# Causal attention in one core: four narrow key tiles of the diagonal are packed in two pairs, and the probability ring grows from three buffers to five

## What is computed

```python
x = x + 0.5 * ffn(layernorm(x))      # 4096 tokens of 128 numbers; a router picks 1 of 8 experts for each
x = x + attn(layernorm(x))           # 4 sequences of 1024 tokens, 16 heads of width 8
x = x + 0.5 * ffn(layernorm(x))

q, k, v = heads(x @ Wq.T), heads(x @ Wk.T), heads(x @ Wv.T)
q, k = rope(q, pos), rope(k, pos)
score = einsum('bqd,bkd->bqk', q, k)
score = where(tril, score, -inf)
out = einsum('bqk,bkd->bqd', softmax(score / sqrt(8)), v) @ Wo.T
```

## Time and profile before

| | |
|---|---|
| median of 3 runs | 908.73 us (904.07 to 913.01) |
| the profiled execution, its own time | 911.38 us |
| its span from first to last instruction | 909.6 us |
| instructions | 17801 |
| mean granted TensorE clock | 0.926 |

### The profile page before, as it was taken

The page is one execution under the profiler, slowest core; times in us unless marked ns, Lnnn a source line. Parts: engine busy times, 40 slices in busy tenths (PEclk is TensorE's granted clock), DMA queues, the critical chain, the costliest instruction groups (busy, mean ns, idle before and its releaser), DMA issues. The chain is left out here.

```text
span 909.6 us, 17801 instructions
## 1 busy us (share of the span) xinstructions
PE 781.4 (86%) x5522; PEld 442.6 (49%) x5570; DVE 615.6 (68%) x1919; ACT 506.6 (56%) x1229; POOL 324.6 (36%) x606
## 2 busy tenths in 40 slices
PE   9757889988889999999999999999999876577795
PEld 8657778654323333333333333333333345476785
DVE  5625467569887788778877887788778419344463
ACT  2125456167337676767676767676767751154462
POOL 7253544546522233223322332233223310535543
PEclk8759899999779999999999999999999988689898
DMA  9511111206550332133213321332130010211100
GB/s 304 212 39 29 38 35 35 110 22 167 158 85 6 54 54 36 19 54 55 35 20 54 55 37 19 54 54 36 20 54 2 3 32 38 92 28 37 39 31 27
DMA packets 27990, 51.84 MB, mean 57 GB/s; under 512 B 7553, under 2 KB 19201, under 8 KB 26497
## 3 DMA queue, kind: packets, MB, share of 16 engines
q1 hardware_dynamic: 21296, 41.04, 19.6%
q0 software_dynamic: 4096, 8.69, 3.6%
q10 hardware_dynamic: 2512, 1.06, 0.5%
HBM read 35.40 MB, written 14.97 MB: 55 GB/s over the span
## 5 line engine op out<-in xcount | busy, mean ns | idle before, releaser
L1456 DVE CUSTOM_DVE_ANT_0 cst<-psS,mask_row 128x768 bf16<-128x768 f32 (+7 forms) x512 | 364.3, 756 | 93.1 <-PE psS L1316 90.6
L1420 ACT ACTIVATE prob<-psST 128x512 f32<-128x512 f32 (+3 forms) x750 | 316.8, 496 | 151.9 <-PE psST L1347 113.3
L1316 PE MATMUL psS<-ks,qs 125*128 125x512 bf16 (+3 forms) x768 | 190.6, 337 | 12.6 <-DVE a_rowmax L1456 12.0
L1347 PE MATMUL psST<-qs,ks 128*128 128x512 bf16 (+3 forms) x703 | 178.9, 324 | 5.3 <-issue 0.4
L1361 PE MATMUL a_psO<-prob,vs 128*32 128x512 f32 (+3 forms) x1536 | 164.1, 499 | 15.8 <-ACT prob L1420 14.6
L1540 POOL TENSOR_TENSOR a_gate<-a_zeros 1x1 f32<-1x1 f32 x128 | 23.4, 183 | 330.5 <-ACT prob L1420 330.5
L1316 PEld LDWEIGHTS psS<-ks,qs 125*128 125x128 bf16 x768 | 56.2, 98 | 162.2 <-DVE a_rowmax L1456 60.5
L1347 PEld LDWEIGHTS psST<-qs,ks 128*128 128x128 bf16 x750 | 68.5, 98 | 99.8 <-ACT prob L1420 49.0
L780 POOL DMA_INDIRECT tok<-rows,f_there_number x64 | 61.6, 963 | 102.0 <-DVE f_number L492 42.4
L729 ACT ACTIVATE f_xnT<-f_ps_half,gb 128x128 f32<-128x128 f32 x64 | 29.3, 457 | 114.2 <-PE f_ps_half L657 57.9
L666 PE MATMUL f_ps_wide<-f_xnT,f_w1s 128*128 x312 | 55.9, 307 | 41.4 <-issue 23.9
(11 more groups left out here) (181 smaller groups left out, 952.7 us busy)
## 6 DMA issues: line engine op xcount, KB each, us to landing
qs<-q_split SPq DMA_DIRECT2D x96, 96.0 KB
rows<-tok SPq DMA_DIRECT2D x8, 536.0 KB, 4.8
ks<-k_split SPq DMA_DIRECT2D x32, 128.0 KB
q_split<-p_part SPq DMA_DIRECT2D x24, 128.0 KB, 2.4
k_split<-p_part SPq DMA_DIRECT2D x24, 128.0 KB, 2.4
ks<-k_split SPq DMA_DIRECT2D x16, 192.0 KB
tok<-x_after_first SPq DMA_DIRECT2D x4, 536.0 KB, 5.2
w<-in_Wb SPq DMA_DIRECT2D x1, 2064.0 KB, 7.9
```

The lines of the kernel that those rows point to most:

```text
L1316: last = nc.tensor.matmul(ps[:, a * CH + c0:a * CH + c0 + w], lhs, ks[r][0:PR, h * S + c0:h * S + c0 + w], start=True, stop=True)
L1347: nc.tensor.matmul(score_buffer(s, m)[:, 0:w], ks[r][:, h * S + j * P:h * S + (j + 1) * P], qs[r][:, q_col(h, q0):q_col(h, q0) + w], start ...
L1420: nc.scalar.activation(prob[:, u % RING, h, 0:w], score_buffer(s, u * QH + h)[:, 0:w], ACT.Exp, scale=SCALE).then_inc(exp_done, 1)
L1456: last = nc.vector.tensor_tensor_reduce(out=out[:, a * CH:a * CH + width], in0=ps[:, a * CH:a * CH + width], in1=mask_row[:, S - width:], ...
```

## The change

- The key tiles with 384 and 128 queries of one chunk (j1 and j3, j5 and j7) become one unit: PE writes both scores side by side into one buffer of 512 columns (two matmuls), and ACT takes one exponential of 512 in place of one of 384 and one of 128. A stage has 10 units for 12, and 40 exponentials for 48. Order of the units: chunk 0: 0 (j0), 1 (j1 and j3), 2 (j2, 256 queries); chunk 1: 3 to 7 (j0 to j4), 8 (j5 and j7), 9 (j6, 256 queries). All PE matmuls stay, the masks too: a pair needs two affine selects behind one gate.
- The probability ring has five buffers. The two new ones lie over buffers that the projection used before; ACT waits, once, until the transfers out of these are done. ACT now waits for W(u-5).
- W(u) stands behind the first score of unit u+2 as before. The copy, which stood on ACT in front of the exponentials of units 1 and 5 (units then counted to 12), now stands in front of those of units 2 and 5 (counted to 10). `EXTRAS` places the transposes behind a given head of a unit.
- In the opening only scores are done, no W any more; W(0), W(1) and W(2) of stage 0 stand in stage 0 itself.
- The score buffers are counted on over the stages (40 scores are no multiple of 3).

```diff
+PB = 5
...
+        for tiles in [(j,) for j in range(j0 + 1)] + [(j0 + 1, j0 + 3), (j0 + 2,)]:
+            pieces, at = [], 0
+            for j in tiles:
+                q0 = max(j * P, ch * CH)
+                pieces.append((j, q0, (ch + 1) * CH - q0, at))
+                at += (ch + 1) * CH - q0
+            units.append((ch, pieces, at))
...
-    half_start = [0, CB]
-    half_end = [CB, UN]
+    half_start = [0, 3]
+    half_end = [3, UN]
+    groups = [(u,) for u in range(UN)]
+    weigh_at = {((u + 2) % UN, 0): u for u in range(UN)}
...
-    EXTRAS = [(1, "turn_max", 1, True), (4, "turn_out", 1, False), (5, "turn_out", 0, True),
-              (7, "turn_max", 0, False)]
+    EXTRAS = [((1, 1), "turn_max", 1, True), ((3, 3), "turn_out", 1, False), ((6, 3), "turn_out", 0, True),
+              ((7, 3), "turn_max", 0, False)]
...
     def exps(s, u):
...
-            wait(act, pv_done, s * UN + u - 2)
+            wait(act, pv_done, s * UN + u - PB + 1)
...
             for u in range(UN):
-                if u == 1 and not first:
+                if u == 2 and not first:
                     copy_out(s - 1, 1)
-                if u == half_end[0] + 1:
+                if u == half_end[0] + 2:
                     copy_out(s, 0)
                 exps(s, u)
...
         def mask(s, u):
...
+            for _, _, _, at in units[u][1]:
+                part = prob[u % PB][:, :, at:at + P]
+                last = nc.gpsimd.affine_select(out=part, in_=part, compare_op=ALU.is_ge, fill=0.0, base=0,
+                                               pattern=[[0, QH], [1, P]], channel_multiplier=-1)
```

More of the change, by code:

```diff
@@ L1114, in attention @@
     for ch in range(NCH):
[L1115 to L1117 removed]
+        j0 = ch * CB
+        for tiles in [(j,) for j in range(j0 + 1)] + [(j0 + 1, j0 + 3), (j0 + 2,)]:
[5 more added lines that the diff above has]
+            units.append((ch, pieces, at))
     UN = len(units)
     SC = UN * QH
[L1120 to L1122 removed]
+    assert UN % PB == 0
+    diagonal = [u for u, (ch, pieces, w) in enumerate(units) if pieces[0][0] * P == pieces[0][1]]
+    half_start = [0, 3]
+    half_end = [3, UN]
+    groups = [(u,) for u in range(UN)]
+    weigh_at = {((u + 2) % UN, 0): u for u in range(UN)}
     tiles = [((h, h + 1), i) for i in range(CB) for h in range(0, QH, 2)]
@@ L1134, in attention @@
     WEIGH_COST = 3
-    att_total = sum((QH + WEIGH_COST) * w for _, _, _, w in units)
+    att_total = sum((QH + WEIGH_COST) * w for _, _, w in units)
+    group_cost = [WEIGH_COST * sum(units[u][2] for u in g) for g in groups]
     def plan(first, last, whole=False):
         found, tile = [], 0
-        att = sum((QH + WEIGH_COST) * w for _, _, _, w in units[:OPEN]) if first and not whole else 0
+        att = sum(QH * w for _, _, w in units[:OPEN]) if first and not whole else 0
         def spread():
@@ L1153, in plan @@
         for u in range(UN):
[L1154 to L1169, removed]
+            for h in range(QH):
+                if not first or u >= OPEN or whole:
+                    found.append(("score", u, h))
+                    att += units[u][2]
+                if (u, h) in weigh_at:
+                    g = weigh_at[u, h]
+                    before = groups[g][0] > u
+                    if not before or not first:
+                        found.append(("weigh", g, int(before)))
+                        att += group_cost[g]
                 spread()
-            for at, what, arg, there in EXTRAS:
-                if at == u and (there or not (first if arg == 1 and what == "turn_out" else last)):
-                    found.append((what, arg, 0))
+                for at, what, arg, there in EXTRAS:
+                    if at == (u, h) and (there or not (first if arg == 1 and what == "turn_out" else last)):
+                        found.append((what, arg, 0))
         att = att_total * 2
@@ L1185, in opening @@
         jobs = jobs[:jobs.index(("score", OPEN, 0))]
-        jobs = [job for job in jobs if job[0] in ("score", "weigh")]
+        jobs = [job for job in jobs if job[0] == "score"]
         for k, (_, what, arg) in enumerate(before_loop[head:]):
@@ L1334, in score @@
         def score(s, r, u, h):
-            ch, j, q0, w = units[u]
+            _, pieces, _ = units[u]
             if u in half_start and h == 0:
@@ L1346, in score, with weigh @@
                 pe.wait_ge(exp_done, s * SC + m - 4)
[L1347 to L1364, removed]
+            for j, q0, w, at in pieces:
+                last = nc.tensor.matmul(score_buffer(s, m)[:, at:at + w], ks[r][:, h * S + j * P:h * S + (j + 1) * P],
+                                        qs[r][:, q_col(h, q0):q_col(h, q0) + w], start=True, stop=True)
+            last.then_inc(scored, 1)
+        def weigh(s, r, g):
+            for u in groups[g]:
+                ch, pieces, _ = units[u]
+                pe.wait_ge(exp_done, s * SC + (u + 1) * QH)
+                if u in diagonal:
+                    pe.wait_ge(masked, s * len(diagonal) + diagonal.index(u) + 1)
+                if u in half_start:
+                    pe.wait_ge(v_ready, s + 1)
+                    wait(pe, out_copied, 2 * s + half_start.index(u))
+                for j, q0, w, at in pieces:
+                    c0 = q0 - ch * CH
+                    for h in range(QH):
+                        last = nc.tensor.matmul(psO[32 * h:32 * h + 32, c0:c0 + w], vs[r][:, j, h, :],
+                                                prob[u % PB][:, h, at:at + w], start=(j == 0),
+                                                stop=(u + 1 in half_end))
+                last.then_inc(pv_done, 1)
         def stage(s, r, turn, first, last):
@@ L1414, in exps @@
         def exps(s, u):
-            ch, j, q0, w = units[u]
-            wait(act, pv_done, s * UN + u - 2)
+            _, _, w = units[u]
+            if s == 0 and u == RING:
+                for i in range(2):
+                    for k in range(2):
+                        act.wait_ge(n.split_stored[i][k], 16 * KINDS * NC8 // 2)
+            wait(act, pv_done, s * UN + u - PB + 1)
             for h in range(QH):
                 act.wait_ge(scored, s * SC + u * QH + h + 1)
-                nc.scalar.activation(prob[:, u % RING, h, 0:w], score_buffer(s, u * QH + h)[:, 0:w], ACT.Exp,
+                nc.scalar.activation(prob[u % PB][:, h, 0:w], score_buffer(s, u * QH + h)[:, 0:w], ACT.Exp,
                                      scale=SCALE).then_inc(exp_done, 1)
```

35 lines of the change are left out of this document (18 added, 17 removed).

## The result

The changed kernel takes 965.32 us (median of 4 runs, 962.10 to 967.54) against 910.87 for the kernel before in the same comparison (904.07 to 913.13): ratio 1.0608, 95% interval 1.0536 to 1.0680. The forecast was 943 and its range ended at 956, so the direction was right and the size was not: +54 us for +34. The profiled execution took 962.1 us; the following is its page.

The account below looks back on a forecast made before the run. PE was taken to bound the kernel, idle 4.3 us of a 30.3 us middle stage; +2.4 us a stage made +34 in 14 stages, 911.4 + 34 = 945, less 2.7 for the median: 943 us, range 920 to 956.

Parts of the forecast that it names:

- Part 1, the pairs: One exponential for two: 0.6 us of ACT a stage, worthless alone; at most 1.6 us of PE idle around narrow units.
- Part 2, the ring: Five probability buffers on ACT: value 0, because PE's list, not the ring, sets the pace.
- Part 3, the copy: W(0) and W(3) on PE wait for ACT's later copy, 1.25 us each: 2.5 us new idle a stage.
- Part 4, the tiles: PE waits at moved tiles: T2, S(1,0), T5, T9 to turn_out1, turn_out0, T19 and turn_max0, 0.2 to 0.9 us each.
- Period: 26.0 + 6.7 = 32.7 us: Middle stage of attention: PE work 26.0 plus idle 6.65, against 30.3 before, +2.4 us a stage.
- some hundredths in five other places: 0.15: Last idle term of PE's middle stage, for small waits outside the named places: 0.15 us together.
- just in time for its W: The pair's mask of 1.5 us ends without delaying its W, since PE has W(7), T22 and T23 meanwhile.
- that any reordering can win: PE's idle time in a middle stage of the kernel before: 4.3 us, 60 us in 14 stages.
- I trust it to about half a us a stage: Accuracy claimed for the walk through PE's list, as the old list landed within 0.1 us at T2, W(0), turn_max0.
- the clock: Rival: PE at half clock for 5 us in every stage, +42 us more, 985 us; chance 0.07.
- The opening with the first stage: First stage: transfer of the maxima some 1.5 us later but less work behind it; within 1 us either way.
- the last stage: Loses about 2 us at the copies, wins about as much at the narrow units: 0, give or take 1.5.

Follow-up runs that it names:

- e5: Changed kernel with the copy in front of units 1 and 4, at most one tile behind a score, none at a transpose; 901.50 us, ratio 0.9945.
- e8_ring3: As e6_early_one_t5, with three probability buffers in place of five; 907.41 us, ratio 1.0008.
- e6_early_one_t5: As e5, with tile T5 moved behind W(0), where the kernel before had it; 907.94 us, ratio 1.0022.
- e2: Changed kernel with only the copy put back one unit earlier on ACT, in front of units 1 and 4; 929.06 us, ratio 1.0201.
- e3: Kernel before with the copy one unit later on ACT, no pairs, three probability buffers; 946.07 us, ratio 1.0390.
- e11: As e4 (late copy, one tile at a time), with tile T5 behind W(0); 937.37 us, ratio 1.0301.
- e4: Changed kernel with at most one tile behind a score and none where a transpose stands, copy left late; 941.37 us, ratio 1.0344.
- e1: Changed kernel with every W one unit later, behind the first score of unit u+3, copy left late; 939.63 us, ratio 1.0298.
- e9: As e1, with at most one tile behind a score; 920.50 us, ratio 1.0116.

## Why the prediction was wrong

**Part 1, the pairs: held in that they are worth little; one reading in it did not hold.** With all else repaired, e5 gains 0.25 us a stage; ACT is busy 20.78 us in a stage for 21.20, 0.4 less where 0.6 was written, and W(9') has no idle of 0.65 in front of it any more. "PE's columns stay, so PE's work stays" is not so: the W of a pair takes 1.00 (467.12 to the next tile at 468.12), and its two halves took 0.79 (449.10 to 449.89) and 0.36 before. Two pairs save 0.3 of PE's work in a stage, about what e5 gains; how much of the 0.25 is this and how much the narrow units' waits was not separated.

**Part 2, the ring: held.** e8_ring3 against e6_early_one_t5 shows no difference, in that order of the work.

**Part 3, the copy: held in place and mechanism, and nearly in size.** The starts are 1.65 apart where 1.6 was written, and counted from starts PE stands 1.32 at each of the two, 2.64 for 2.5. Taken back, they give 1.9 (e2), and put into the old kernel 2.15 for 2.4 (e3).

**Part 4, the tiles: held in place and in size.** Counted in the same way PE stands 0.78 at T2, 0.31 by W(9'), where S(1,0) was named, 0.81 at T5, 0.72 at T9, T10 and turn_out1, 0.51 at turn_out0, 0.80 at T19 and turn_max0: 3.93, where 4.0 was written.

**The step that failed is the sum: "Period: 26.0 + 6.7 = 32.7 us", and in it the term "some hundredths in five other places: 0.15".** The period is 33.50. Its work, counted from starts, is 26.06, so 26.0 held. Its idle time is 7.44 where 6.65 was written: 2.64 at the copies, 3.93 in part 4, and 0.87 for the 0.15. This 0.87 stands in front of the other seven W, 0.08 to 0.21 each. W(1) starts at 467.12, where T7 (0.44) and a score (0.22) from 466.31 on would be done at 466.97. W(8') at 456.71 waits for POOL, 0.27 as shown and 0.21 by starts: the pair's mask did not end "just in time for its W". W(5) starts 0.31 behind a score of 0.22 (480.89, 481.20) and no idle is shown there. The kernel before has the same 0.31:

```profile
462.17 0.38 PE L1347 MATMUL psST<-qs,ks 128*128 128x512 bf16 x1
462.48 1.06 PE L1361 MATMUL a_psO<-prob,vs 128*32 128x512 f32 x8
```

So going from a score to a W takes some 0.09 here, also where nothing is waited for; what takes it was not looked for. The prediction had it nowhere: it counted work from starts and idle from the named waits, and in the kernel before this 0.09 went into the 4.3 of idle time "that any reordering can win". 0.8 us a stage more than written is 11 us in 14 stages. "I trust it to about half a us a stage" was too narrow: three places of the old list that come out right don't bound the sum of a whole period.

**The rival that came true in part was the clock,** given 0.07 as a case where every stage pays 3 us. It came in four stages of 14 and took 1.56 each, 6.2 us in the profiled execution. The argument against it, "single gaps of at most 1.25 with work between", didn't hold, nor did it help that no stretch is idle as a whole: in all four, gaps of 0.65 and 1.16, with 0.83 us of busy PE between them as shown, stood in front of W(0). Both gaps seem to be needed: with T5's gap gone (e11) or the copy's (e2) no middle stage of the profile had a spell, and e4, which has both, had three. But the same two gaps stand in all 14 stages, and ten of them ran at the full clock; what picks the four is open. (The row of 425 to 430, PE busy 3.20, already reaches into W(0); the last section has the stages side by side.)

**Smaller terms.** The opening with the first stage was 0.8 longer (within 1 was written); what lies ahead of it was 4.1 shorter, which is not the change's doing; the last stage was 1.9 longer (0 give or take 1.5), PE standing 2.04 and 1.60 for its copies; what follows was 1.2 longer. In sum: 11 from the period and 6 from the clock, and the ends cancel; that is the 17 us between +34 and the +50.8 of the profiled span. Some 5 us more between 943 and 965 are the choice of execution: the median was put 2.7 under the profiled one, and it lies 3.2 above it. Without the clock's 6 us the time would still lie beyond 956.

## What to carry to other kernels

When a copy sits on one in-order engine between the last and the first use of an accumulator, keep a whole unit of other work between it and the instruction that waits, on both engines; having the copy one unit later cost 2 us a stage here, with or without the rest of the change. Moving the W one unit later instead (e1, e9) brought other waits. When units are merged, look again at everything placed by unit number: the saving was 0.25 us a stage and the moved neighbours cost 3.5. A hand walk finds the large waits and sizes them; its sum misses what each hand-over costs, so measure the hand-overs too (0.09 from a score to a W here, ten times a stage), and let a whole period of the old kernel come out of the walk before trusting the new one.

## What the runs showed of the hardware

The clock of TensorE fell to its lower level in middle stages of the change and of e4_one_tile, though no single gap was long. It fell only where two waits, 0.65 for a tile and 1.16 for the copy, stood close together; with either one gone (e2_copy_early, e11_late_t5), and also in e3_late_copy_before with 1.54 and 0.88 far apart, it stayed at 1.00. And it fell in 4 stages of 14 that were alike before it: in the five us that end with the start of W(0), PE was busy 3.16 or 3.17 in every one of the 14, at a granted clock of 1.00. So these waits together make a fall possible and don't decide it; no run here shows what does. The Trainium skill, page "TensorE: Matmul & The Clock Gate", section "HAM oscillation — how this bites in real kernels", tells of a loop in which a wait for a transfer throttles the clock again in every single round. This trace is not that case: the waits were for other engines, none was longer than 1.3 us counted from starts, and only some rounds were hit.
